# An audio tower on one core: context, fold, logits and sums of lengths in smaller tiles of TensorE

## The reference

```
# 1: merge 750 tokens to 375
h = gelu(x @ W1 + b1); h = gelu(h @ W2 + b2)
new_lens = sigmoid(h @ W3 + b3);  new_lens *= (T / 2) / sum(new_lens)
h = warp(x, new_lens)                      # interpolation weights @ x
# 2: linear attention, 8 heads of 64 channels, 8 memory keys and values
q, k, v = split(rmsnorm(layernorm(h)) @ w_qkv)
q = softmax(q, over channels) * scale;  k = softmax(k, over keys)
context = einsum('bhdn,bhen->bhde', k, v)  # 64 x 64 per head, 383 keys
out = einsum('bhde,bhdn->bhen', context, q) @ w_out + b_out
h = h + rmsnorm(out)
# 3: switch layer, 16 experts, capacity by order of arrival
logits = layernorm(h) @ switch_w.T + switch_b
h = h + (chosen expert, or the token itself over capacity) * probability
```

## Time and profile before

| | us |
|---|---|
| median of 3 runs | 429.95 (428.99 to 430.51) |
| profiled execution | 429.19 |
| its span, first to last instruction | 427.2 |
| period of the row pipeline (start of one context to the next, six times) | 43.0 |

### The profile page before, as it was taken

The page is one execution under the profiler, slowest core; times in us unless marked ns, Lnnn a source line. Parts: engine busy times, 40 slices in busy tenths (PEclk is TensorE's granted clock), DMA queues, the critical chain, the costliest instruction groups (busy, mean ns, idle before and its releaser), DMA issues.

```text
span 427.2 us, 7511 instructions
## 1 busy us (share of the span) xinstructions
PE 395.6 (93%) x2463; PEld 350.1 (82%) x2463; DVE 345.3 (81%) x930; ACT 216.6 (51%) x428; POOL 150.1 (35%) x198
## 2 busy tenths in 40 slices
PE   3898899999999999999999999999999696999891
PEld 2776688998889888988898889888988596999791
DVE  4457757877999799889987998799879974796795
ACT  3625527851885178517951794279427621771000
POOL 4100130103156404640464046404640471005782
PEclk9999999999999999999999999999999888999898
DMA  6374030001000100010001000100000008132134
GB/s 191 86 229 150 2 93 0 2 2 43 0 2 20 43 1 2 20 43 2 0 21 44 0 2 18 43 1 2 21 0 1 2 18 186 47 98 65 34 78 124
DMA packets 21076, 18.49 MB, mean 43 GB/s; under 512 B 5010, under 2 KB 17656, under 8 KB 20734
## 3 DMA queue, kind: packets, MB, share of 16 engines
q1 hardware_dynamic: 17054, 15.23, 13.0%
q0 software_dynamic: 2880, 2.35, 2.4%
q10 hardware_dynamic: 1104, 0.44, 0.4%
HBM read 11.33 MB, written 6.62 MB: 42 GB/s over the span
## 4 chain that ended last, share of the span: by engine, by line
PE 72%; issue 7%; POOL 6%; ACT 6%; DMA 5%; DVE 3%; POOLq 1%; ACTq 0%; SPq 0%; DVEq 0%
PE psB L948 10%; PE psB L949 10%; PE psB L947 10%; PE psC L973 7%; PE psC L1064 4%; PE psC L910 4%; PE psC L911 4%; PE psC L912 4%; PE psC L1081 4%; ACT h L642 3%; POOL h L601 2%; PE psC L1050 2%; PE psA L910 2%; DMA h2b<-slot_x 1%; ACT kT L629 1%
## 5 line engine op out<-in xcount | busy, mean ns | idle before, releaser
L947 PE MATMUL psB<-W2h,h1l 128*125 128x512 f32 x192 | 78.9, 411 | 0.0
L948 PE MATMUL psB<-W2l,h1h 128*125 128x512 f32 x192 | 76.2, 397 | 0.0
L949 PE MATMUL psB<-W2h,h1h 128*125 128x512 f32 x192 | 76.2, 397 | 0.0
L653 ACT ACTIVATE h2b<-h2b 125x512 f32<-125x512 f32 x48 | 30.0, 626 | 48.9 <-DVE h2b L1410 48.9
L642 ACT ACTIVATE h<-psA,b1c 128x376 f32<-128x376 f32 x64 | 35.6, 577 | 20.8 <-PE psA L912 20.8
L1410 DVE TENSOR_TENSOR h2b<-psB,b2r 125x512 f32<-125x512 f32 x48 | 33.0, 687 | 15.1 <-PE psB L949 14.8
L949 PEld LDWEIGHTS psB<-W2h,h1h 128*125 128x125 f32 x192 | 35.8, 187 | 9.1
L947 PEld LDWEIGHTS psB<-W2h,h1l 128*125 128x125 f32 x192 | 36.1, 188 | 7.5 <-DVE h1l L1401 0.3
L948 PEld LDWEIGHTS psB<-W2l,h1h 128*125 128x125 f32 x192 | 36.0, 188 | 7.2
L1401 DVE TENSOR_TENSOR h1l<-h,h1h 128x1504 fp32r<-128x1504 f32 x16 | 27.5, 1720 | 14.6 <-ACT h1h L629 14.6
L518 POOL TENSOR_TENSOR sg<-euler,sg 125x6 f32<-125x6 f32 x8 | 10.7, 1336 | 75.3 <-DVE sg L1424 75.3
(11 more groups left out here) (267 smaller groups left out, 999.4 us busy)
## 6 DMA issues: line engine op xcount, KB each, us to landing
xt<-in_x SPq DMA_DIRECT2D x8, 336.0 KB
slot_x<-eb_parts SPq DMA_DIRECT2D x2, 960.0 KB, 9.0
basef<-in_L_tok_W SPq DMA_DIRECT2D x1, 1024.0 KB, 7.2
ewf<-slot_x SPq DMA_DIRECT2D x2, 480.0 KB, 6.0
h2b<-slot_x SPq DMA_DIRECT2D x2, 480.0 KB, 7.8
slot_y<-h SPq DMA_DIRECT2D x4, 240.0 KB, 2.5
slot_y<-A SPq DMA_DIRECT2D x4, 240.0 KB, 3.1
qa<-in_L_attn_w_qkv SPq DMA_DIRECT2D x1, 768.0 KB
```

The costliest lines, as they stand in the source:

```text
L653: nc.scalar.activation(slot, slot, ACT.Gelu).then_inc(c_g2.sem, 1)
L947: mm(ps, lo, W2h[:, k, :], start=k == 0, stop=False)
L948: mm(ps, hi, W2l[:, k, :], start=False, stop=False)
L949: last = mm(ps, hi, W2h[:, k, :], start=False, stop=k == HK - 1)
```

## The change

- The context is made head by head: for each i of 4 and each key tile, one matmul for head i into partitions 0 to 63 of psC0 and one for head 4 + i into partitions 64 to 127, both with 64 weight columns and 64 moving columns. 24 matmuls (48 passes) where 12 (24) were. The blocks that weren't wanted are no longer made.
- `cbd` is 128 x 4 x 64, with heads 0 to 3 on the lower and 4 to 7 on the upper partitions; one copy of 128 x 256 fills it. Its memset and `c_cba` are gone.
- `wo` is laid out in the same way, by two DMAs of half the size.
- The fold is one matmul per head, weights 64 x 64 and moving 64 x 128: 8 matmuls (16 passes) where 4 (8) were. Heads 0 to 3 write psC1 and heads 4 to 7 psC3, each on the partitions that `m` has for the head. As psC3 also holds the sums, the fold waits for `c_csn`.
- `take_m` is two operations, one for each bank.
- The sums and the logits are split by output partitions 0 to 63 and 64 to 124: 4 matmuls where 2 were, and 6 where 3 were.
- The order of calls in each `step` and in `ending` stays as it was.

```diff
-        cbd = sb("cbd", [128, PAIRS, 128])
+        cbd = sb("cbd", [128, HEADS // 2, D])
...
+        HALVES = (0, 1)
+        TOK_HALVES = (slice(0, D), slice(D, TP))
+        def head(half, i):
+            h = half * HEADS // 2 + i
+            return slice(h * D, (h + 1) * D)
+        def bank_fold(half):
+            return psC[1] if half == 0 else psC[3]
...
-                             (wo[:], w_out.rearrange("(p k) c -> k p c", k=128)),
+                             (wo[0:D], w_out[0:HID // 2].rearrange("(i e) c -> e i c", e=D)),
+                             (wo[D:128], w_out[HID // 2:HID].rearrange("(i e) c -> e i c", e=D)),
...
-            pool.memset(cbd[:], 0.0).then_inc(s_const, 1)
...
-                copy(cbd[D:128, :, D:128], psC[0][D:128, :].rearrange("p (a d) -> p a d", a=PAIRS)[:, :, D:128]).then_inc(c_cba.sem, 1)
-                copy(cbd[0:D, :, 0:D], psC[0][0:D, :].rearrange("p (a d) -> p a d", a=PAIRS)[:, :, 0:D]).then_inc(c_cbd.sem, 1)
+                copy(cbd[:].rearrange("p i d -> p (i d)"), psC[0][:, 0:HEADS // 2 * D]).then_inc(c_cbd.sem, 1)
...
-                mm(psC[3][0:TP, 0:1], tri[:], pre[:, TJ - 1:TJ], start=True, stop=True)
-                mm(psC[3][0:TP, 1:2], parts[:], pre[:, TJ - 1:TJ], start=True, stop=True).then_inc(c_cs.sem, 1)
+                for col, w in enumerate((tri, parts)):
+                    for p in TOK_HALVES:
+                        last = mm(psC[3][p, col:col + 1], w[:, p], pre[:, TJ - 1:TJ], start=True, stop=True)
+                last.then_inc(c_cs.sem, 1)
...
-                for p in range(PAIRS):
-                    d = slice(p * 128, (p + 1) * 128)
+                for i in range(HEADS // 2):
                     for j in range(KJ):
                         n = KEYS[j].stop - KEYS[j].start
-                        last = mm(psC[0][:, d], v[0:n, j, d], kT[0:n, j, d], start=j == 0, stop=j == KJ - 1)
+                        for half in HALVES:
+                            d = head(half, i)
+                            last = mm(psC[0][half * D:(half + 1) * D, i * D:(i + 1) * D], v[0:n, j, d], kT[0:n, j, d], start=j == 0, stop=j == KJ - 1)
                 last.then_inc(c_ctx.sem, 1)
...
-                for p in range(PAIRS):
-                    last = mm(psC[1][:, p * C:(p + 1) * C], cbd[:, p, :], wo[:, p, :], start=True, stop=True)
+                if f is not None:
+                    after(pe, c_csn, f, 1)
+                for i in range(HEADS // 2):
+                    for half in (i % 2, 1 - i % 2):
+                        rows, to = slice(half * D, (half + 1) * D), slice(i % 2 * D, (i % 2 + 1) * D)
+                        last = mm(bank_fold(half)[to, i // 2 * C:(i // 2 + 1) * C], cbd[rows, i, :], wo[rows, i, :], start=True, stop=True)
                 last.then_inc(c_m.sem, 1)
...
                 for j in range(GJ):
-                    last = mm(bank_lg(b)[0:TP, j * E:(j + 1) * E], xf_turned(b)[:, j * TP:(j + 1) * TP], swT[:], start=True, stop=True)
+                    for p in TOK_HALVES:
+                        last = mm(bank_lg(b)[p, j * E:(j + 1) * E], xf_turned(b)[:, j * TP + p.start:j * TP + p.stop], swT[:], start=True, stop=True)
...
-                vec.tensor_tensor(m[:], psC[1][:].rearrange("p (a c) -> p a c", a=PAIRS),
-                                  rk[:].unsqueeze(2).to_broadcast([128, PAIRS, C]), ALU.mult).then_inc(c_ms.sem, 1)
+                for half in HALVES:
+                    p = slice(half * PAIRS // 2, (half + 1) * PAIRS // 2)
+                    last = vec.tensor_tensor(m[:, p], bank_fold(half)[:, 0:PAIRS // 2 * C].rearrange("p (a c) -> p a c", c=C),
+                                             rk[:, p].unsqueeze(2).to_broadcast([128, PAIRS // 2, C]), ALU.mult)
+                last.then_inc(c_ms.sem, 1)
```

More of the change, by code:

```diff
@@ L124, in audio_tower @@
         mvT = sb("mvT", [NM, HID])
-        wo = sb("wo", [128, PAIRS, C])
+        wo = sb("wo", [128, HEADS // 2, C])
         bor = sb("bor", [TP, C])
@@ L266, in audio_tower @@
         c_qt = counted("c_qt", 3); c_qtc = counted("c_qtc", 3)
-        c_ctx = counted("c_ctx", 1); c_cba = counted("c_cba", 1); c_cbd = counted("c_cbd", 1)
+        c_ctx = counted("c_ctx", 1); c_cbd = counted("c_cbd", 1)
         c_m = counted("c_m", 1); c_rk = counted("c_rk", 1); c_ms = counted("c_ms", 1)
@@ L1046, in q_transposed @@
                 if j == 0:
-                    after(pe, c_cba, b, 1)
                     after(pe, c_cbd, b, 1)
@@ L1059, in context, with fold @@
                     pe.wait_ge(s_mem, 16)
-                for p in range(PAIRS):
-                    d = slice(p * 128, (p + 1) * 128)
+                for i in range(HEADS // 2):
                     for j in range(KJ):
                         n = KEYS[j].stop - KEYS[j].start
-                        last = mm(psC[0][:, d], v[0:n, j, d], kT[0:n, j, d], start=j == 0, stop=j == KJ - 1)
+                        for half in HALVES:
+                            d = head(half, i)
+                            last = mm(psC[0][half * D:(half + 1) * D, i * D:(i + 1) * D], v[0:n, j, d], kT[0:n, j, d], start=j == 0, stop=j == KJ - 1)
                 last.then_inc(c_ctx.sem, 1)
-            def fold(b, prev):
-                after(pe, c_cba, b, 1)
+            def fold(b, prev, f):
                 after(pe, c_cbd, b, 1)
                 after(pe, c_qtc, b, 2)
-                for p in range(PAIRS):
-                    last = mm(psC[1][:, p * C:(p + 1) * C], cbd[:, p, :], wo[:, p, :], start=True, stop=True)
+                if f is not None:
[4 more added lines that the diff above has]
+                        last = mm(bank_fold(half)[to, i // 2 * C:(i // 2 + 1) * C], cbd[rows, i, :], wo[rows, i, :], start=True, stop=True)
                 last.then_inc(c_m.sem, 1)
@@ L1230, in step @@
                     q_transposed(k, before(k), 2)
-                    fold(k, before(k))
+                    fold(k, before(k), f)
                 if f is not None and k is not None:
@@ L1326, in ending @@
                 dense(k, 0)
-                fold(f, k)
+                fold(f, k, None)
                 q_transposed(f, k, 2)
@@ L1913, in _ @@
             pipeline(dve, step, ending, setup)
-N_CONST = 17
-N_WR = 12
+N_CONST = 16
+N_WR = 13
 N_PREP = 8
```

## The result

The changed kernel takes 424.55 us (median of 4 runs, 423.59 to 426.07) against 430.06 for the kernel before on the same chip: a ratio of 0.9879, 95% interval 0.984 to 0.9917. Measured once more, in another batch, the same kernel gave 426.00 us and 0.9905 [0.9868, 0.9941]. The second measurement, 426.00, would lie just inside it; the steps, at 42.53 us each, are the same in both, and not the forecast's.

What follows compares the result with a forecast made beforehand. PE's queue was taken to bound each step until a wait appears. Context -0.50, sums -0.01, fold +0.20, logits -0.06 and shape changes +0.33 gave -0.04 us a step, six times -0.2: 429.7 us against 429.95, range 425 to 438.5.

Steps and rivals of the forecast that it cites:

- What bounds the kernel: Row pipeline: PE's queue sets the 43.00 us step; context, folds and logits count six times, in the ending nearly nothing.
- the fold with its change of shape: Fold in each step: +0.20 us for its passes and +0.15 for changing rows and columns of the tile.
- Length of one small pass: PE: 0.057 us for 64 columns of weights and moving data, 0.112 us for 128 moving columns.
- How they combine: Context: second pass of a pair waits 0.057 us, next tile's pair 0.03; 0.087 a pair, 24 pairs, 2.16 us.
- Sums: Sums behind the context, 4 passes to 8: 0.36 us to 0.35, taken as -0.01 us a step.
- Fold: Fold, 8 passes to 16 with 128 moving columns: 0.93 us to 1.13, +0.20 us a step.
- Logits: Logits, 6 passes to 12: 0.58 us to 0.52, -0.06 us a step, at most 0.15 to gain.
- Changing the tile shape: Three visits to smaller tiles a step: 0.15 us for the fold, 0.09 for each other visit, +0.33 us.
- (a): Rival: tiles overlap fully and shape changes are free; -0.80 us a step, 425.2 us, chance 0.33.
- (b): Rival: nothing overlaps between the tiles; +1.45 us a step, 438.6 us, chance 0.18.
- (c): Rival: overlap as forecast, but each shape change waits for PE's pipeline, 0.3 us a visit; 433 us, chance 0.07.
- Off the path: ScalarE's cbd copy, DVE's take_m, the fold's wait for c_csn, wo's transfers and the dropped memset: all at nothing.

Runs made afterwards that it cites:

- fold alone: The kernel before with only the fold made per head, in two diagonal 64 x 64 tiles; 428.10 us, ratio 0.9972.
- the sums later: The changed kernel with sums behind queries 0 and 1 and the warp waiting for two of three query copies; 424.00 us, ratio 0.9861.
- the order experiments: The changed kernel with passes reordered: fold tile by tile 426.26 us, context by half 429.86 us, context by head 425.98 us.

## Why the forecast was wrong, step by step

**What bounds the kernel: right.** Work on PE was worth its length until a wait came, and the wait came where PE's queue met DVE and ScalarE. Counting the context's steps six times was right as well.

**The step that failed: the fold with its change of shape, +0.20 and +0.15 us a step in the forecast.** With the fold undone the period is the same (42.51 against 42.53), so together they are worth 0. That is 0.35 of the 0.43 us by which the forecast of a step was off. Two things were wrong in it: how passes of several tiles combine, and that I looked for no wait behind the fold. The rest is mainly the change of shape around the context, +0.09 forecast, which a wait covers too.

**Length of one small pass: right, 0.057 and 0.11 us. How they combine: wrong.** I let the second pass of a pair hold back the next tile, as if PE took its queue strictly in order, and so had 0.087 us a pair and a context of 2.16 us. It is 1.40, under even my lower bound of 1.51: a pass of another tile starts while the pair is still at work. For the context this cost the forecast nothing, because I had capped its gain by the scan: -0.50 forecast, -0.45 measured, as the sums start 0.10 us behind the scan's end and not 0.05.

**Sums: -0.01 forecast, -0.04 measured** (0.36 to 0.32).

**Fold: +0.20 forecast, 0 measured, for two reasons that I missed.** First, how passes combine: not 1.13 us but four tiles at once, 0.40 from first to last start, which is under the lower bound of 0.90. That bound assumed that the stream of 128 columns can't be shared. With two tiles instead of four (fold alone) it is 0.82, and the period gets 0.22 us longer with the change of shape in it, where my terms for the fold had +0.35; the 0.18 us more from queries to warp are mostly change of shape, as the passes themselves take 0.82 instead of 0.78. Second, a wait that I did not look for. From the last queries' transposes to the warp it is 1.36 us in the kernel before (219.87 - 218.51), in the changed one (217.75 - 216.39) and with the fold undone (216.18 - 214.82). The warp waits for the third query copy. This row of the kernel before stood in the trace and not among mine:

```profile
219.14 0.59 ACT L629 ACTIVATE qT<-psC 128x500 f32<-128x500 f32 x1 [0.93 <-PE psC L1050]
```

It ends at 219.73, 0.14 us ahead of the warp at 219.87. No idle time is drawn before the warp there, because the old fold was just as long as the wait. I named the clip (218.84) as what is late next, and had 1.03 us of room where there was 0.04, by the kernel before with the wait shortened.

**Logits: -0.06 forecast without their change of shape; -0.04 measured with it.** From first to last start they fell from 0.46 to 0.31; the gap ahead of them grew from 0.17 to 0.26, which is the price of the change of shape.

**Changing the tile shape: +0.33 forecast, about +0.09 paid.** The price was nearly right: 0.09 on entry of the logits, 0.20 us from the last queries' pass to the fold where 0.11 is usual, 0.09 again from the fold's last pass to the warp where no wait covers it (0.20 with the sums later, 0.11 with the fold undone besides), and 0.10 more within the warp, for which I had nothing. But the context's entry lies behind a wait for kT that is 0.22 us with either shape, the way out behind the sums is in their 0.32 us, and those of the fold are behind the query copy. I summed a price for each place and asked at none of them whether a wait covers it.

**The sum.** By the measured terms -0.45 - 0.04 + 0 - 0.04 = -0.53 a step; the period fell by 0.47. The forecast had -0.04. The gap is the fold (0.20) and the visits (0.24, of them 0.15 the fold's). The other terms come out 0.05 better than forecast, and the sum is 0.06 better than the period; of that, 0.02 lies in the first transposes behind the sums and 0.02 in the first matmuls behind the logits.

**The rivals.** (a), tiles overlap fully, is the mechanism that the trace shows; its 425.2 was close to the result, but its step of -0.80 was not: -0.47, since it too gave the fold and the logits more than the waits allow. That the total came near was luck: besides the steps it is the entry of the ending and the differences of clock and start-up between executions. (b), nothing overlaps, fell with the first row of the context; for the page of the Trainium skill that spoke for it, see the order experiments. The Trainium skill's page "TensorEngine Tiling (Array Packing)", Overview, had up to 2x for one small dimension and more for both; measured 1.9 for the context (2.64 to 1.40) and 1.95 for the fold (0.78 to 0.40), which halves both dimensions but also needs twice the passes. (c), 0.3 us a visit, fell: 0.09.

**Off the path: right.** The copy into `cbd` is one of 0.40 us; `take_m` is two of 0.42, and nobody waits for it; the fold never waits for `c_csn`.

## What to carry to other kernels

Cost small matmuls per tile of the array, passes in that tile times the pace of one, and take the longest tile, not the sum; interleave tiles every few passes: where tiles share their rows, the other one starts when three passes of the first are still to come (1.53 us for groups of six, 2.58 for groups of 24). Add a change of shape on the way in and out, 0.1 to 0.2 us each here, unless a wait covers it. Before crediting a shorter group on a full queue, subtract the next instruction's own releaser: the producer's end, searched for on every engine, even where no idle time is drawn today, since the work that you shorten may be exactly what hides it. When a cut turns into a wait, move the waiting instruction behind work that needs nothing: here that gave as much again as the change itself, and 0.04 us a step without it.

## What was not expected of the hardware

- Four 64 x 64 tiles stream 128 columns each at the same time, their passes starting some 7 ns apart; two 64-column tiles on the same 128 rows alternate at 0.029 us a pass.
- PE starts a pass of a free tile ahead of earlier ones in its queue whose tile is busy. Between the two column halves it does so when three earlier passes have not started: groups of six cost 1.53 us against 1.40, groups of 24 cost 2.58.
- In the ending the granted clock differs between executions of one kernel, 1.00 and 0.88, which is 2 us of the total. What sets it was not tried.
